# Edge counts packed as three-bit digits, a last layer that sums over edges before its weights, and softmax sums shared with GpSimd

## The reference

```
L0  q, k, v = h@Wq+bq, h@Wk+bk, h@Wv+bv                       # 8 heads of 64
    scores where an edge exists, else -1e9; softmax over the QUERY axis; @v; @Wo+bo
    h1 = LN(h + .)*g1+be1 ; LN(h1 + relu(h1@W1+b1)@W2+b2)*g2+be2
L1  h@wc + mean over edges of (h@wn) + bias
L2  4 experts of two layers each, relu(mean_edges(h)@Wl + bl + h@Wr), the best 2 of 4 by a softmax gate
L3  H = X@W + b
    src_f, dst_f = edges plus one loop per node
    deg[n] = number of (edges + loop) that end in n ;  isd = 1/sqrt(deg)
    out = relu(segment_sum(H[src_f] * isd[src_f] * isd[dst_f], dst_f))
```

## Time and profile before

| | |
|---|---|
| median of 3 runs | 519.67 us (519.45 to 520.11) |
| profiled execution, its own time | 517.47 us |
| its span, first to last instruction | 515.7 us |
| granted TensorE clock, mean | 0.974 of full speed |
| busy share of the span: PE, PEld, DVE, ACT, POOL | 90%, 66%, 62%, 39%, 30% |
| chain that ended last, by engine | PE 60%, DVE 21%, ACT 9%, issue 5%, POOL 4%, DMA 1% |

### The profile page before, as it was taken

The page is one execution under the profiler, slowest core; times in us unless marked ns, Lnnn a source line. Parts: engine busy times, 40 slices in busy tenths (PEclk is TensorE's granted clock), DMA queues, the critical chain, the costliest instruction groups (busy, mean ns, idle before and its releaser), DMA issues.

```text
span 515.7 us, 6318 instructions
## 1 busy us (share of the span) xinstructions
PE 462.6 (90%) x2235; PEld 341.5 (66%) x2235; DVE 319.4 (62%) x630; ACT 202.5 (39%) x258; POOL 155.5 (30%) x100
## 2 busy tenths in 40 slices
PE   3999899688887899969979999999999999999794
PEld 2467444233344787847858888888888888888582
DVE  5999982899995888594496224622362336232846
ACT  4989833545413242135162224123413341333223
POOL 3000000011011696429360433443344334433100
PEclk9899999999988999989998999999999999999898
DMA  8840000000011123302201024202420332010002
GB/s 255 242 168 0 2 2 20 1 0 1 1 51 51 42 81 123 147 16 104 81 10 74 0 90 135 102 1 107 159 83 5 133 128 81 10 72 1 0 1 82
DMA packets 22476, 34.36 MB, mean 67 GB/s; under 512 B 5680, under 2 KB 5936, under 8 KB 22448
## 3 DMA queue, kind: packets, MB, share of 16 engines
q1 hardware_dynamic: 22160, 33.85, 19.4%
q10 hardware_dynamic: 288, 0.13, 0.1%
HBM read 32.93 MB, written 1.05 MB: 66 GB/s over the span
## 4 chain that ended last, share of the span: by engine, by line
PE 60%; DVE 21%; ACT 9%; issue 5%; POOL 4%; DMA 1%; ACTq 0%; SPq 0%; DVEq 0%
PE ps L1106 15%; PE ps L1107 15%; PE ps L1108 15%; PE ps L1170 4%; ACT distance L541 3%; DVE rsum L867 3%; PE ps L1134 3%; PE ps L1135 3%; PE ps L1177 2%; ACT one_dst L546 2%; DVE e_sb L365 2%; DVE stats L684 2%; DVE half_sum L863 2%; POOL x_sb L469 1%; PE ps L1119 1%
## 5 line engine op out<-in xcount | busy, mean ns | idle before, releaser
L444 POOL TENSOR_TENSOR w_lo<-w_stage,w_hi 128x1024 fp32r<-128x1024 f32 x22 | 52.7, 2393 | 137.6 <-ACT w_hi L511 137.6
L511 ACT ACTIVATE w_hi<-w_stage 128x2048 fp32r<-128x2048 f32 x23 | 43.9, 1909 | 73.0 <-PE ps L1108 73.0
L445 POOL TENSOR_TENSOR w_lo<-w_stage,w_hi 128x1024 fp32r<-128x1024 f32 x22 | 57.4, 2607 | 0.0
L1107 PE MATMUL ps<-w_lo,hid_hi 128*128 128x512 f32 x128 | 49.9, 390 | 0.0
L1106 PE MATMUL ps<-w_hi,hid_hi 128*128 128x512 f32 x128 | 49.9, 390 | 0.0
L1108 PE MATMUL ps<-w_hi,hid_lo 128*128 128x512 f32 x128 | 49.9, 390 | 0.0
L1039 DVE TENSOR_SCALAR tmp<-ps,bl 128x512 f32<-128x512 f32 x16 | 12.0, 751 | 52.1 <-ACT hid_hi L646 52.1
L1106 PE MATMUL ps<-T_hi,w_hi 128*128 128x512 f32 (+1 forms) x112 | 41.5, 371 | 1.8 <-DVE T_lo L713 1.4
L1107 PE MATMUL ps<-T_lo,w_hi 128*128 128x512 f32 (+1 forms) x112 | 41.0, 366 | 0.0
L1108 PE MATMUL ps<-T_hi,w_lo 128*128 128x512 f32 (+1 forms) x112 | 40.9, 365 | 0.0
L453 POOL TENSOR_TENSOR w_lo<-w_stage,w_hi 128x512 fp32r<-128x512 f32 x4 | 5.1, 1264 | 106.2 <-DVE rsum L865 106.2
(11 more groups left out here) (188 smaller groups left out, 1094.6 us busy)
## 6 DMA issues: line engine op xcount, KB each, us to landing
w_stage<-in_L_gnn_Wr SPq DMA_DIRECT2D x8, 1024.0 KB, 5.2
w_stage<-in_L_gnn_Wl SPq DMA_DIRECT2D x8, 1024.0 KB, 5.2
w_stage<-in_L_gnn_W SPq DMA_DIRECT2D x5, 1024.0 KB, 6.3
x_sb<-in_x SPq DMA_DIRECT2D x4, 256.0 KB, 3.7
w_q<-in_L_gnn_Wq SPq DMA_DIRECT2D x1, 1024.0 KB, 7.5
w_k<-in_L_gnn_Wk SPq DMA_DIRECT2D x1, 1024.0 KB, 9.9
w_v<-in_L_gnn_Wv SPq DMA_DIRECT2D x1, 1024.0 KB, 5.6
w_o<-in_L_gnn_Wo SPq DMA_DIRECT2D x1, 1024.0 KB, 8.7
```

The source lines that it names most:

```text
L444: gp.tensor_tensor(w_lo[s][:, 0:2], stage[s][:, 0:2], f32(w_hi[s][:, 0:2]), ALU.subtract)
L445: gp.tensor_tensor(w_lo[s][:, 2:4], stage[s][:, 2:4], f32(w_hi[s][:, 2:4]), ALU.subtract)\
L511: nc.scalar.activation(w_hi[u % 2][:], stage[u % 2][:], ACT.Copy).then_inc(hi_made, 1)
L1107: nc.tensor.matmul(goal, a_hi, b_lo, start=False, stop=False, **kw)
```

## The change

1. **Counts.** Eight counts of three bits replace six of four. dst is cut into quarters (rows of `one_dst` have 128 numbers in place of 256), src into halves (rows of `one_src` have 256 in place of 172). A group takes eight matmuls with 256 columns in place of 16 with 172. VectorE makes its four `one_dst` of a group in one comparison of two tensors, ScalarE makes its four as before with half the numbers. The index arithmetic ahead uses shifts and masks. The two copies of T_sb that VectorE made, and the four of k_sb, go to ScalarE. The order of TensorE's groups among the q and k tiles changes, and TensorE waits for k_sb later.
2. **Softmax sums.** From the second step on GpSimd adds heads 0 and 1 to heads 2 and 3 (512 numbers, result `pool_sum`), started when the exponentials of the first four heads are there and the sum of the step before is ready. VectorE adds heads 4, 5 to 6, 7 (512 numbers), then `pool_sum` (512), then the last 256. GpSimd's former small jobs go ahead of the steps or behind them, and the power that gives `isd` goes there as well.
3. **Last layer.** The normalisation also divides by the root of the degree (`vareps` is multiplied by `deg_1`). TensorE sums the normalised rows over edges, loop included (`loop_hi`, counts plus a diagonal), straight into the transposed layout: tiles 0 and 1 in plain float32, tiles 2 and 3 as hi and lo. That result is split and multiplied by W3. The bias enters as `b3 * reach`, where `reach` is the sum of isd over the edges, worked out early with 16 matmuls of two columns. The four transposes, the bias additions and the `isd` scalings of H are gone.

```diff
-    THIRD = 172
-    DIGIT = 4
+    DIGIT = 3
+    ONE = 127 - 9
...
@@ GpSimd
-            for i in range(STEPS):
-                gp.wait_ge(sums_made, i + 1)
-                if i < DT:
-                    split_lo_tile(W1A, i)
-                else:
-                    add_row(BO, i - DT, h_sb, bo_added)
+            gp.wait_ge(digits_made, 1)
+            add_row(BO, 0, h_sb, bo_added)
+            gp.wait_ge(ct_ready, 1)
+            for k in range(DT):
+                split_lo_tile(W1A, k)
+            for i in range(1, STEPS):
+                e = e_bufs[i % E_BUFS]
+                gp.wait_ge(exp_done, 2 * i + 1)
+                gp.wait_ge(sums_made, i)
+                gp.tensor_tensor(pool_sum[:], e[:, 0:2], e[:, 2:4], ALU.add).then_inc(pool_half, 1)
+            gp.wait_ge(sums_made, STEPS)
+            add_row(BO, 1, h_sb, bo_added)
+            gp.wait_ge(prob_done, 2 * STEPS)
+            add_row(BO, 2, h_sb, bo_added)
+            add_row(BO, 3, h_sb, bo_added)
+            gp.wait_ge(pow_ask, 1)
+            gp.tensor_tensor(isd[:], deg_1[:], half_neg.to_broadcast([P, NT]), ALU.pow).then_inc(pow_made, 1)
...
@@ ScalarE
-                        last = nc.scalar.activation(distance[:, s, :], iota_n[:, 0:HALF], ACT.Abs,
-                                                    bias=edge_neg[:, bass.ds(c, 1)])
+                        last = nc.scalar.activation(distance[:, s, :], iota_n[:, 0:P], ACT.Abs, scale=-1.0,
+                                                    bias=edge_m[:, 1, bass.ds(c, 1)])
...
-            for t in (0, 2):
+            for t in range(NT):
...
+            for j in range(PAIRS):
+                act.wait_ge(k_done, j + 1)
+                nc.scalar.activation(k_sb[:, j, :], ps[:, k_bank(j), :], ACT.Identity, bias=bk[:, j:j + 1])\
+                  .then_inc(k_made, 1)
...
+            act.wait_ge(reach_done, 1)
+            nc.scalar.activation(reach_2[:], ps[:, 7, 0:2 * NT].rearrange("p (t w) -> p t w", t=NT), ACT.Copy)\
+              .then_inc(reach_out, 1)
...
+                if e == 0:
+                    nc.scalar.activation(loop_hi[:], f32(c_hi[:]), ACT.Copy).then_inc(loop_copied, 1)
...
                 normalise(LN5, t, h_sb, x_sb, ACT.Relu)
-                transposed_hi(T5, 0, t)
-            for t in range(NT):
-                act.wait_ge(H_made, t + 1)
-                nc.scalar.activation(R_hi[:, t, :], tmp[:, t, :], ACT.Copy).then_inc(H_hi_made, 1)
+                if t >= WHOLE:                                  # WHOLE = 2
+                    act.wait_ge(ln_out, ln_out_no(LN5, t))
+                    nc.scalar.activation(R_hi[:, t, :], h_sb[:, t, :], ACT.Copy).then_inc(last_hi_made, 1)
+            for j in range(DT):
+                act.wait_ge(mix_done, j + 1)
+                nc.scalar.activation(agg_hi[:, j, :], ps[:, j, :], ACT.Copy).then_inc(mix_hi_made, 1)
...
@@ VectorE, index arithmetic and one-hots
-            link(nc.vector.tensor_copy(edge_f[:], edge_i[:]))
...
-            nc.vector.tensor_scalar(neg_ident[:], ident[:], -1.0, None, ALU.mult).then_inc(neg_made, 1)
+            link(nc.vector.tensor_scalar(inner[:, 0, :], edge_i[:, 0, :], HALF - 1, None, ALU.bitwise_and))
+            link(nc.vector.tensor_scalar(inner[:, 1, :], edge_i[:, 1, :], P - 1, None, ALU.bitwise_and))
+            nc.vector.tensor_copy(edge_m[:], inner[:]).then_inc(onehot_act, 1)
+            link(nc.vector.tensor_copy(inner_dst[:], inner[:, 1, :]))
...
+                    own = UN - ACT_CHUNKS
+                    chunks, slots = bass.ds(g * UN + first, own), bass.ds(g * UN + first % RING, own)
+                    nc.vector.tensor_tensor(one_dst[:, slots, :],
+                                            iota_n[:, 0:P].unsqueeze(1).to_broadcast([P, own, P]),
+                                            inner_dst[:, chunks].unsqueeze(2).to_broadcast([P, own, P]), ALU.is_equal)
                     for s in range(UN):
...
-                        if s < UN - ACT_CHUNKS:
-                            nc.vector.tensor_scalar(one_dst[:, bass.ds(slot, 1), :].squeeze(1), iota_n[:, 0:HALF],
-                                                    edge_m[:, 1, bass.ds(c, 1)], None, ALU.is_equal)
-                        last = nc.vector.tensor_scalar(one_src[:, bass.ds(slot, 1), :].squeeze(1), iota_n[:, 0:THIRD],
+                        last = nc.vector.tensor_scalar(one_src[:, bass.ds(slot, 1), :].squeeze(1), iota_n[:, 0:HALF],
...
-            for t in (1, 3):
-                v.wait_ge(tr_done, tr_no(T0, t))
-                nc.vector.tensor_copy(T_sb[:, :, t * P:(t + 1) * P], ...).then_inc(T_made[1], 1)
...
-            for j in range(PAIRS):
-                v.wait_ge(k_done, j + 1)
-                nc.vector.tensor_scalar(k_sb[:, j, :], ps[:, k_bank(j), :], bk[:, j:j + 1], None, ALU.add)\
-                  .then_inc(k_made, 1)
...
+            for digit in range(2 * NT):
+                half, quarter = digit // NT, digit % NT
+                last = nc.vector.tensor_scalar(digits[:, quarter, half * HALF:(half + 1) * HALF], packed[:],
+                                               DIGIT * digit, 2 ** DIGIT - 1 if digit < 2 * NT - 1 else 2 ** 24 - 1,
+                                               ALU.logical_shift_right, ALU.bitwise_and)
...
@@ VectorE, softmax
-                link(nc.vector.tensor_tensor(half_sum[:], e[:, 0:4], e[:, 4:8], ALU.add))
-                link(nc.vector.tensor_tensor(half_sum[:, 0:2], half_sum[:, 0:2], half_sum[:, 2:4], ALU.add))
+                if i == 0:
+                    ...                                          # as before
+                else:
+                    link(nc.vector.tensor_tensor(half_sum[:, 0:2], e[:, 4:6], e[:, 6:8], ALU.add))
+                    v.wait_ge(pool_half, i)
+                    link(nc.vector.tensor_tensor(half_sum[:, 0:2], half_sum[:, 0:2], pool_sum[:], ALU.add))
...
@@ VectorE, last layer
+            for t in range(WHOLE, NT):
+                v.wait_ge(last_hi_made, t - WHOLE + 1)
+                nc.vector.tensor_tensor(R_lo[:, t, :], h_sb[:, t, :], f32(R_hi[:, t, :]), ALU.subtract)\
+                  .then_inc(last_lo_made, 1)
+            for j in range(DT):
+                v.wait_ge(mix_hi_made, j + 1)
+                nc.vector.tensor_tensor(agg_lo[:, j, :], ps[:, j, :], f32(agg_hi[:, j, :]), ALU.subtract)\
+                  .then_inc(mix_lo_made, 1)
...
-                nc.vector.tensor_tensor(tmp[:, t, :], ps[:, t, :], tmp[:, t, :], ALU.add).then_inc(last_sum, 1)
+                nc.vector.scalar_tensor_tensor(tmp[:, t, :], b3_row[:], reach[:, t:t + 1], ps[:, 4 + t, :],
+                                               ALU.mult, ALU.add).then_inc(last_sum, 1)
...
@@ TensorE
-                        for m in range(2):
-                            last = nc.tensor.matmul(ps[:, 7, m * THIRD:(m + 1) * THIRD],
-                                                    one_dst[:, s, m * P:(m + 1) * P], one_src[:, s, :],
+                        last = nc.tensor.matmul(ps[:, 7, 0:HALF], one_dst[:, s, :], one_src[:, s, :],
...
-            for j, ready in enumerate((0, 1, 2, 2)):
+            for j, ready in enumerate((1, 1, 2, 2)):
...
-            for j, ready in enumerate((3, 3, 3, 2)):
+            for j, ready in enumerate((2, 2, 3, 3)):
...
-            pe.wait_ge(k_made, PAIRS)                            # ahead of the v tiles; now behind them
...
+            for k in range(NT):
+                if k < WHOLE:
+                    pe.wait_ge(ln_out, ln_out_no(LN5, k))
+                else:
+                    pe.wait_ge(last_lo_made, k - WHOLE + 1)
+                ...
+                for j in range(DT):
+                    if k < WHOLE:
+                        nc.tensor.matmul(ps[:, j, :], h_sb[:, k, col(j)], f32(loop_hi[:, k, :]), start=k == 0,
+                                         stop=False)
+                        continue
+                    nc.tensor.matmul(ps[:, j, :], R_hi[:, k, col(j)], loop_hi[:, k, :], start=False, stop=False)
+                    last = nc.tensor.matmul(ps[:, j, :], R_lo[:, k, col(j)], loop_hi[:, k, :], start=False,
+                                            stop=k == NT - 1)
+                    if k == NT - 1:
+                        last.then_inc(mix_done, 1)
...
+            for t in range(NT):
+                last_rows(t, 0)                                  # waits for agg_lo 0, then one mm3
+            for t in range(NT):
+                for j in range(1, DT):
+                    last = last_rows(t, j)
+                last.then_inc(last_done, 1)
```

181 lines of the change are left out of this document (101 added, 80 removed).

## The result

The kernel after takes 497.70 us (median of 4 runs, 497.21 to 497.99), the kernel before, timed beside it, 519.56 us (519.26 to 520.11). The ratio is 0.9577, 95% interval 0.9561 to 0.9594.

The account below looks back on a forecast made before the run. VectorE was taken to bound the counts and softmax, TensorE the experts, which the change leaves alone. Terms -6.6 - 3.6 + 0.4 - 6.6 = -16.4 gave a median of 503.3 us, own range 501 to 505.5, wider range 498.5 to 507.

Parts of the forecast that it names:

- the sum of a group on VectorE: Counts, groups behind the first ring: comparison, `one_src` spacing and end gap add up to 3.07 us a group, not 3.33.
- this cancels: Counts, first ring: one 0.62 us comparison replaces four `one_dst` at 0.20, eight `one_src` grow 0.02; four groups stay about 11.8 us.
- the counts: Stage up to the first v tile: VectorE stays the bound, v tiles start at 61.1 in place of 67.73, 6.6 us less.
- Two numbers a cycle: Rival for VectorE's merged comparison in the counts: it runs at the 16-bit rate, 4.3 us less, 499.0 us; chance 0.09.
- Wider spacing: Rival in the counts: VectorE's `one_src` spacing grows with the numbers, 2.9 us more, 506.7 us with the seams; chance 0.11.
- the slow branch: Rival: a node pair with eight edges or more sets `slow_flag`, counts are made again, above 620 us; chance 0.01.
- GpSimd's addition: Rival in the softmax sums: it starts late, collides with VectorE's scaling and is no help, 507.0 us; chance 0.06.
- The clock in the last layer: Rival: TensorE's clock falls there after all, with a drop around the layer's weights 2.4 us, 505.7 us; chance 0.08.
- Softmax: Softmax sums: in seven steps VectorE's 1024-wide addition becomes 512, 0.526 us each, less a tenth for the wait; 3.6 us less.
- Behind the last step: After the last softmax scaling: GpSimd's two `bo` additions and power delay VectorE by 0.4 us, between 0 and 1.
- the work on `reach`: Second layer: 16 matmuls and a small copy delay its first normalised tile some 2 us, hidden by TensorE's later idle time.
- Last layer: Last layer to the end: last VectorE instruction ends at 506.6 instead of 513.2, 6.6 us less, half work gone, half clock.

Follow-up runs that it names:

- experiment 1: Kernel before with VectorE's one-hot loops written out, so the same 12 instructions per group have constant addresses; 517.92 us, ratio 0.9983.
- experiment 2: Kernel after with VectorE's one-hot loops written out, so its nine instructions per group have constant addresses; 497.58 us, ratio 0.9596.
- experiment 3: Kernel after with VectorE's one comparison of 4 x 128 numbers cut back into four instructions of 128; 506.58 us, ratio 0.9776.
- experiment 4: Kernel before with only VectorE's four comparisons of 256 numbers per group merged into one of 4 x 256; 518.79 us, ratio 1.0015.
- experiment 5: Kernel after without GpSimd's additions in the softmax, VectorE adding all eight heads itself; 500.80 us, ratio 0.9654.
- experiment 7: Kernel after with the last count transposes and third W_o tile put before the two normalised tiles' transposes on TensorE, behind the softmax; 493.76 us, ratio 0.9521.
- experiment 6: Kernel after with GpSimd's three late additions of bo and its power for isd moved earlier, away from the end of the softmax; 497.84 us, ratio 0.9603.
- experiment 9: The kernel of experiment 7 unchanged, timed once more; 494.90 us, ratio 0.9527.
- experiment 12: Kernel after with all four node tiles of the last layer split into high and low parts, none in full float32; 503.72 us, ratio 0.9715.
- experiment 8: Kernel after with the changes of experiment 6 and experiment 7 together; 494.10 us, ratio 0.9537.

## Why the prediction was wrong, point by point

**The step that failed** is the sum of a group on VectorE: "0.62 + 7 x 0.26 + 0.34 + the gap of 0.29 that now ends a group", with the remark on the first ring that "this cancels". The comparison and the spacing in it were right. The gap was carried over as if it belonged to the loop. It belongs to issue: VectorE's queue falls behind by the instructions that make addresses, and it shows only where these take longer than the execution of what they feed. Twelve short instructions didn't cover them, nine with one of 0.68 us did (experiments 1 to 3). That is 12 x (3.07 - 2.655) = 5.0 us. Of the 0.41 us a group, 0.29 are the gap. Another 0.08 are the 0.34 counted for the last `one_src`, where the next comparison now starts 0.26 behind it; the rest is size. In the first ring the same: before, its groups started 2.67, 2.86 and 3.11 us apart as issue fell behind, which I averaged over; after, 2.655 each, 10.6 in place of 11.8 us. Together 6.2 us, of which 6.0 arrive at the v tiles; the rest of the counts (start, 0.95 us behind VectorE, TensorE near to being the bound) was right. The prediction had asked whether the spacing was "issue of instructions" and answered yes; it then didn't ask what fewer instructions do to it.

**Rivals.** Two numbers a cycle is out: 0.68 us for 512 numbers, and 1.21 for 1024 in experiment 4. The Trainium skill, "Vector Engine (DVE) Microarchitecture Reference", section 5.1, where one element read 16 times as either source of such an instruction ran at the single rate, agrees with this row (128 times here); the tier table of the Trainium skill's "VectorE: DVE Perf Modes", read alone, would not. Wider spacing is out, the slow branch was not taken. GpSimd's addition was of help, 1.26 to 1.27 us in each step. The clock in the last layer held.

**Softmax: -3.1, not -3.6.** The mechanism was right, seven times 0.53 us (experiment 5). 0.41 were lost to one wait for the scores, behind a fall of the clock; where the clock held in this step, in experiment 7, there was no such wait. 0.15 were lost where one `pool_sum` (128.20) ran into a scaling, which took 2.51 us instead of 2.36.

**Behind the last step: +1.2, not +0.4.** GpSimd's queue cost 0.5 as worked out (0.4). The other 0.7 is where the clock fell: before's profiled run had its fall late, and other runs of the same program show 8.96 and 9.05 us in place of its 8.30 (experiment 6). The sum had no term for that; whether the longer idle time makes the fall come earlier is not shown. At W1 the loss stands at 1.3 us (17.24 against 15.96). The rest of the +1.8 I read only from the traces. The first normalised tile of the second layer comes 2.0 us later behind W1 (52.48 against 50.52), as the prediction had for the work on `reach`, and all but 0.3 of it is covered by the third layer's first (89.26 against 88.98). Another 0.3 comes up to the last layer's first; its cause is open.

**Last layer: -6.0, not -6.6.** Right in each step: TensorE starts at 467.97, 0.15 us behind the tile, and ends without a fall of the clock. The missing half microsecond lies ahead of the product with the weights: it begins 12.7 us behind the start of the first normalised tile (479.73 - 467.01), worked out were 12.1.

**The median.** -16.4 missed 3.6 of the 20.0 us of the profiled runs: the 6.0 of the counts, less 2.5 by which the other three terms came out smaller than forecast. So the total is nearer than its largest term, and that is luck. The other 1.9 us are the place of before's profiled run below its median; with the 20.0 us alone the median would be 499.6 us, inside the range. In later series the kernel before had medians from 517.7 to 519.3 us.

## What to carry to other kernels

When instructions with moving addresses are merged or dropped, ask first whether their spacing is issue. Here the gap marked "issue" stood where one instruction executes in 0.22 us on average (2.67 / 12, experiment 1) and costs 0.277 to issue, and it was gone at 0.295 (2.655 / 9); nothing between was measured. And the gain on one engine appeared only when the other engine of the pair was freed too. Before moving a job on a queue, list what it will then stand in front of, not only what it stands behind. Where an engine stands still for microseconds while other ready work waits on its own queue, change the order: that brought some 3 to 4 us here, and taking GpSimd's jobs out of the way (experiment 6) nothing that can be told.

## What the runs showed of the hardware

- A VectorE instruction of 256 f16 numbers with one pointer (a number per row, read from memory) follows in 0.20 us when its address is a constant, one of 172 with two pointers in 0.24 (experiment 1), one of 256 with two in 0.26 (experiment 2). In loops of twelve with addresses from registers they stand 0.24 to 0.25 apart in the later rings of the kernel before, and 0.22 to 0.26 with 128 and 256 numbers (experiment 3), plus 0.21 to 0.30 at the end of a loop. In loops of nine (the kernel after) the same addresses cost nothing.
- A VectorE comparison of two f16 operands, one of them one number repeated 128 or 256 times, took 0.68 us for 512 numbers (the kernel after) and 1.21 for 1024 (experiment 4), as long as a float32 addition of as many (0.69 and 1.22).
- The same idle time of TensorE did and did not bring the lower clock. After 2.90 us in one and the same kernel, four matmuls took 1.04 us in one execution (clock 1.00, experiment 7) and 1.89 in another (0.50, experiment 9). After 3.9 us, four transposes took 1.11 us in the kernel after and 0.66 in experiment 12, with the same program up to there.
- At the start of the experts the clock fell without TensorE standing still: in experiment 9 it had been at 1.00 until 255 us, TensorE had run the gate's products with 4 columns each, one every 0.11 us, from 252.90 on, and from 256 to 258 us it is at 0.50. From the third layer's first normalised tile to the last layer's it took 222.8 us in the kernel after and in experiment 8, 226.1 in experiments 7 and 9, with the same instructions. Single executions of a version spread by some 4.5 us (491.4 to 495.9 in experiment 7); how much of that this stretch makes is not shown.
